# A new order in the prologue of an attention and FFN kernel, with identity matmuls on TensorE beside it

## The reference

```
x = x + attention(layernorm(x), ctx, ctx, WQ, WK, WV, WO, mask)
x = x + ffn(layernorm(x), W1, b1, W2, b2)
layernorm(x) = (x - mean) / sqrt(var + 1e-5)
attention: Q = x.WQ, K = ctx.WK, V = ctx.WV; softmax(Q.K / 8 + mask * -1e9).V; heads side by side, times WO
ffn: gelu(qlinear(y, W1, b1)), then qlinear(., W2, b2)
qlinear: activations rounded to 8 bits by their global minimum and maximum, weights by their largest magnitude
```

## Time and profile before

| | |
|---|---|
| median of three runs | 1129.66 us |
| the profiled execution's own time | 1126.18 us |
| its span, first to last instruction | 1124.1 us |
| mean granted clock of TensorE | 0.977 |
| busy: TensorE, DVE, ScalarE, POOL | 1018.1, 978.2, 865.1, 770.6 us |
| busy in 5 to 22 us of the prologue (17 us): TensorE, DVE, ScalarE, POOL | 4.91, 11.88, 7.66, 4.20 us |

### The profile page before, as it was taken

One profiled execution on the slowest core, in us unless ns is written; L12 is line 12 of the kernel. 1 busy time (PEld: TensorE's weight loads), 2 busy tenths in 40 slices (PEclk: granted clock), 3 DMA queues, 4 the chain that ended last, 5 costly groups with the idle time before them and its releaser, 6 DMA issues.

```text
span 1124.1 us, 37431 instructions
## 1 busy us (share of the span) xinstructions
PE 1018.1 (91%) x10489; PEld 643.3 (57%) x10489; DVE 978.2 (87%) x2528; ACT 865.1 (77%) x1805; POOL 770.6 (69%) x1108
## 2 busy tenths in 40 slices
PE   3999999999999999999999999999999999985808
PEld 2555566666666666666666666666666666653307
DVE  5777999999999999999999999999999999973997
ACT  4555888888888888888888888888888888873916
POOL 2246877777777777777777777777777777773700
PEclk9999999999999999999999999999999999996969
DMA  8301665555555555555555555555555555555003
GB/s 253 113 1 31 130 134 131 131 135 135 135 135 131 130 135 132 130 131 134 135 135 135 135 135 135 132 130 130 134 135 135 132 130 130 134 132 153 1 0 117
DMA packets 441419, 138.22 MB, mean 123 GB/s; under 512 B 413650, under 2 KB 440374, under 8 KB 441398
## 3 DMA queue, kind: packets, MB, share of 16 engines
q1 hardware_dynamic: 441398, 137.96, 51.0%
HBM read 28.60 MB, written 6.55 MB: 31 GB/s over the span
## 4 chain that ended last, share of the span: by engine, by line
PE 75%; DVE 10%; ACT 5%; issue 4%; POOL 3%; DMA 1%; DVEq 1%; ACTq 0%; SPq 0%; POOLq 0%
PE front L341 19%; PE front L343 17%; PE front L342 17%; PE back L1226 8%; PE front L1208 6%; PE tp L1208 5%; POOL hl L585 3%; DVE hrange L1059 2%; DVE hrange L1060 2%; DVE prob L939 2%; ACT prob L711 2%; DVE k_l L959 1%; ACT q_h L749 1%; PE front L1291 1%; ACT ctx_h L745 1%
## 5 line engine op out<-in xcount | busy, mean ns | idle before, releaser
L585 POOL TENSOR_TENSOR hl<-prob,hl 100x361 f16<-100x361 f32 x512 | 432.1, 853 | 97.2 <-DVE hl L946 50.9
L711 ACT ACTIVATE prob<-prob,nmax 100x361 f32<-100x361 f32 x512 | 293.9, 587 | 47.7 <-DVE nmax L939 47.5
L341 PE MATMUL front<-ctx_h,wk_h 128*128 128x362 f16 x512 | 164.2, 321 | 31.3 <-POOL ctx_l L574 17.8
L1226 PEld LDWEIGHTS back<-v,pT 128*128 128x128 f16 (+1 forms) x4608 | 165.1, 98 | 45.1 <-issue 9.6
L717 ACT ACTIVATE hl<-prob 100x361 f16<-100x361 f32 x352 | 176.0, 500 | 7.9
L1226 PE MATMUL back<-v,pT 128*128 128x65 f16 (+1 forms) x4608 | 174.2, 194 | 6.3 <-DMA pT<-hl 6.2
L343 PE MATMUL front<-ctx_h,wk_l 128*128 128x362 f16 x512 | 161.7, 316 | 0.0
L342 PE MATMUL front<-ctx_l,wk_h 128*128 128x362 f16 x512 | 161.5, 315 | 0.0
L721 ACT ACTIVATE k_h<-front 128x362 f16<-128x362 f32 x256 | 118.9, 464 | 54.7 <-PE front L343 54.7
L959 DVE SCALAR_TENSOR_TENSOR k_l<-front,k_h 128x362 f16<-128x362 f32 x256 | 135.2, 528 | 24.4 <-ACT k_h L721 21.8
L939 DVE CUSTOM_DVE_ANT_0 prob<-front,mask_g,ngain 100x361 f32<-100x361 f32 x256 | 149.6, 584 | 2.2
(11 more groups left out here) (180 smaller groups left out, 1980.8 us busy)
## 6 DMA issues: line engine op xcount, KB each, us to landing
ctx_raw<-ctxT SPq DMA_DIRECT2D x33, 361.0 KB, 3.1
pT<-hl SPq DMA_TRANSPOSE x256, 3.1
xs<-x SPq DMA_DIRECT2D x8, 400.0 KB
q_all<-x SPq DMA_DIRECT2D x32, 100.0 KB
out<-q_all SPq DMA_DIRECT2D x32, 100.0 KB
xb<-out SPq DMA_DIRECT2D x5, 640.0 KB, 7.5
out<-xb SPq DMA_DIRECT2D x25, 128.0 KB, 1.8
q_all<-wq SPq DMA_DIRECT2D x1, 1024.0 KB, 6.6
```

Source lines behind the costliest of these rows:

```text
L341: eng.matmul(dst, lh, rh, start=first, stop=False)
L585: pool.tensor_tensor(hl[0:T, n % RT, 1, 0:S], prob[0:T, n % RP, 0:S], hl[0:T, n % RT, 0, 0:S], ALU.subtract).then_inc(s_lo, 1)
L711: act.activation(prob[0:T, n % RP, 0:S], prob[0:T, n % RP, 0:S], ACT.Exp, bias=nmax[0:T, n:n + 1], scale=-1.0).then_inc(s_exp, 1)
L1226: ins = pe.matmul(obank[j % 2][:, n % GH * DV:(n % GH + 1) * DV], pT[0:r, n % RT, part_ * ST + st, :], v2[half][0:r, st, v, n % HT, :], st ...
```

## The change

DVE's instructions at the start of the prologue get another order: the maxima of WQ and its unit come in front of chunk 1's statistics, and x's low halves in front of WQ's first low half. TensorE gets 128 more matmuls of the float16 identity by itself, 128 columns each, into bank `tp[1]`, which nothing uses until chunk 1: 80 ahead of the transposes of chunk 0, 8 ahead of `top_w(0)`, 24 behind it, and 16 more once the first high half of WQ is there. Nothing reads what they write. The other engines' code is unchanged.

```diff
@@ DVE @@
         stats_x(0)
         dve.wait_ge(s_st, TB)
         ln_moments(chain(dve, s_lv), dve, 0)
-        stats_x(1)
         abs_w(0, 0)
         abs_w(0, 1)
         unit_w(0)
-        low_w(0, 0)
+        stats_x(1)
         start(dve, (s_k, s_v, s_cm, s_cr, s_sv, s_max, s_mg, s_hv, s_ri, s_nrm, s_x1, s_ln))
         x_low(0, 0)
+        low_w(0, 0)
         low_w(0, 1)
         stats_x(2)
@@ TensorE @@
+        def warm_up(times):
+
+            for _ in range(times):
+                pe.matmul(tp[1][:, 0:P], identb[:, :], identb[:, :], start=True, stop=True)
+
+        warm_up(80)
         x_transposes(0, 0)
+        warm_up(8)
         top_w(0)
+        warm_up(24)
+        pe.wait_ge(s_whi, 1)
+        warm_up(16)
         for c in range(NB):
             q_chunk(c, c % 2, c < NB - 1)
```

## The result

The changed kernel takes 1130.63 us (median of 20 runs, 1128.71 to 1132.09), the kernel before 1129.0 us in 20 runs beside them. The ratio is 1.0018 (95% interval 1.001 to 1.0025): it is slower, by 1.6 us as the difference of the medians and 2.0 us by the ratio. That is clear of zero; the ratio lies just inside the 0.2% that the prediction took as its bound, and its interval reaches beyond it. The profiled execution has a span of 1128.6 us and a mean granted clock of 0.974, against 1124.1 us and 0.977 before. About half of this difference of the clocks is one of bookkeeping: over the first 30 us the column has 0.94 after and 1.00 before, though the rows of before show nine matmuls at the low level there.

A forecast was written before the change was run, and what follows sets the result against it. TensorE's chain of waits (75%) bounds the kernel, so its exit from the prologue counts: 1.0 (m = 2 later) + 1.9 (clock) = +2.9 us, +2.3 against the median 1129.66, giving 1132.0 us; 8 in 10 from 1128.9 to 1133.9.

The forecast's parts named there:

- the rival given 0.13: Clock low at chunk 0's transposes: maximum at 14.6 instead of 13.3, m = 2 1.3 us later, 1133.3 us; chance 0.13.
- POOL held: POOL's steps for chunk 1 blocked beside WQ's two low halves on DVE, ending at 21.1 instead of 19.2 alone.
- The four terms of the prediction's sum: POOL's last four steps for chunk 1, 0.28 + 0.28 + 1.11 + 0.2 us from 19.1, said to end at 21.1.
- the upper bound of 22.35: Latest end of POOL's steps for chunk 1, if x's low halves on DVE block POOL too.
- m = 2: Projection's third output block, waits for ScalarE's copy of block 0: 0.8 to 1.1 us later than 22.80, taken 1.0.
- The clock falls: TensorE's clock falls in its 3.8 us wait before m = 2, costing 1.45 to 2.7 us, taken 1.9.
- the row of 4.09 us: Old profile: TensorE stood 4.09 us before a matmul at 1010.81, and the granted clock had fallen by then.
- not blocked enough: POOL ends at 19.2, TensorE waits 2.0 us and keeps its clock, m = 2 1.05 us earlier, 1128.0 us; chance 0.12.
- the luck of the profile of before: Profiled old prologue had an early clock rise; otherwise it loses up to 1.2 us more, 0.6 in the middle.
- the forecast's case: POOL blocked, m = 2 1.0 us later, clock falls in the wait for 1.9 us: 1132.0 us; chance 0.55.
- The case with the clock held: POOL blocked but TensorE's clock holds in the wait: only 1.0 us lost, 1130.1 us; chance 0.17.
- the gain arrives whole: TensorE starts projection 1.6 us earlier at full clock, 3.1 us gained, copy of block 0 by 19.8, 1126.0 us; chance 0.03.

The follow-up runs named there:

- experiment 1: Only the identity matmuls added to the kernel before, DVE's order as before; 1126.58 us, ratio 0.9985 to the kernel before.
- experiment 3: Changed kernel with 60 more identity matmuls ahead of m = 2, in TensorE's wait; 1130.24 us, ratio 1.0016 to the kernel before.
- Experiment 5: Changed kernel with WQ's low halves on DVE reading one input from a zeroed PSUM tile instead of SBUF; 1126.75 us, ratio 0.9984 to the kernel before.
- experiment 4: Changed kernel with chunk 1's statistics moved between WQ's maxima and WQ's unit on DVE; 1125.6 us, ratio 0.9976 to the kernel before.
- experiment 2: Changed kernel without any identity matmuls, so DVE's new order alone; 1130.59 us, ratio 1.0019 to the kernel before.
- experiment 6: Changed kernel with chunk 1's statistics ahead of WQ's unit and no identity matmuls; 1127.35 us, ratio 0.9992 to the kernel before.

## Why the prediction was right, step by step

1. **WQ's maxima** from 8.2 to 10.5: measured 8.23 to 10.57.
2. **80 matmuls** between 4.3 and 8.5 us, hidden: 6.91 us, to 8.95, 2.8 us ahead of the transposes. They raise the clock.
3. **The scale** ready at 14.15: its reciprocal ran from 14.02 to 14.18. This rests on the fast clock at the transposes (0.91 us). The clock was high there in both profiles of the changed kernel. In those of experiments 1, 3 and 5 it had fallen by the transposes of the maxima (0.63 to 0.69 us instead of 0.39), and in that of experiment 4 just behind them; so the rival given 0.13 does occur, in part, in kernels whose TensorE has the same work up to there (experiments 3 and 5); how often it does in the changed kernel itself is not known.
4. **Statistics** at 14.1 to 15.5: 14.10 to 15.48.
5. **Projection** from 17.75: 17.77. WQ's low halves were done at 18.83 (18.9).
6. **POOL held** beside the low halves, shift at 21.1: it ended at 21.13. The agreement to 0.03 us is luck. The four terms of the prediction's sum, from 19.1, give 20.97 and not 21.1. Three steps were done in front of the first held one, not four, so one more step of 0.28 us stood behind the low halves; and POOL went on from 18.97, 0.13 us earlier than taken. x's low halves let POOL through: three steps from 15.56 to 16.33 ran beside them at 0.20 to 0.21 us, so the upper bound of 22.35 falls and the Trainium skill's rule agrees here too. Experiment 5 shows the mechanism, with 1.98 us for the hold; the forecast's own difference was 1.9 us (21.1 less 19.2).
7. **m = 2** 1.0 us later: 0.88 later (22.80 to 23.68).
8. **The clock falls** with the wait: shown. Price taken 1.9 us, measured 1.68 us (3.72 less 2.04, experiment 3), or 1.69 against the kernel before's own 2.03. One of the two rows from which the fall was argued was misread. The row at 1020.85 was taken as a clock that held through 2.27 us, but it was low before that wait (columns as in the earlier trace rows):

```profile
1017.00:1018.00 1.00, 1.00 (x7) 0.95 (x6) 0.00 (x0) 0.09 (x1) 0.67 (x1) 0.50 0.00 0
...
1019.00:1020.00 1.00, 0.00 (x0) 0.00 (x0) 0.11 (x1) 0.00 (x0) 0.00 (x0) 1.00 0.83 190
```

It rose at about 1018.9, in the wait itself, and the row says nothing of a clock that holds. The rows that do are in the new profiles: behind a wait of 2.81 us the transposes of the changed kernel still ran at the high level (0.91 us), and so did m = 2 behind 1.73 us in experiment 5. The forecast's choice between fall and hold thus stood on the row of 4.09 us alone, and the kept clock in the price of the rival "not blocked enough" had no row behind it.

The sum against the profile: 0.88 + 1.69 = 2.57 us, where 2.9 was forecast, and it passes the loop whole. (The spans of the two profiles differ by 4.5 us; the rest is 0.2 us in the loop and 1.7 us behind it.) **Mis-sized terms.** Both of the above by 0.1 and 0.2 us; and the luck of the profile of before, taken as 0.6 us. The second profile of before is 1.58 us later at chunk 1's transposes, so half of this, 0.8 us, is the better figure. At L821 the means of two profiles each are 95.75 before and 97.34 after: 1.6 us. That is also the measured difference of the medians, where 2.3 was forecast; with two profiles of each kernel, and stretches behind the loop that differ by up to 3 us, so close an agreement is partly luck. The rest of the 1.4 us between 1132.0 and 1130.63 is the starting point: 1129.66 was the median of three runs, and 20 runs have 1129.0.

The chances: the forecast's case came true in its mechanism, and the result lies just under the bound of 0.2% that split this case between same and slower. The case with the clock held fell with the rows behind m = 2 in both profiles of the changed kernel. The case "not blocked" fell with the rows of POOL; "the gain arrives whole" needed the statistics earlier on DVE and the copy of block 0 by 19.8; experiment 4 gives it both, and has 5.8 us at L821 against the changed kernel.

The prediction's sentence that all of the gain is lost in the wait is borne out by experiments 1 and 2: the matmuls are worth 1.3 us at L821 with the old order (against the first profile of before), 1.9 to 2.0 us where POOL gets its input early, and 0.2 us in the changed kernel.

## What to carry to other kernels

When a step of one engine is moved ahead of another, the step that was passed now runs beside new neighbours: ask who waits for it and what will run beside it, since small steps of POOL took 1.26 and 1.11 us instead of 0.20 beside DVE instructions with two SBUF inputs. A gain at the start of TensorE's work is only kept if the next tile that it must wait for comes earlier too, and a wait of 3.7 us cost another 1.7 us through the clock. Put the small producer of a long chain (statistics, POOL, ScalarE) in front, and only then the long work.

## What had not been expected of the hardware

- Executions of one program differ by the moments at which TensorE's clock rises: 1.6 us in the prologue of the kernel before and, together with a lower clock, 3.1 us behind its loop, as large as the whole effect of the change. The profile's own time (1126.18 before) was an early rise, and the same parts in several profiles were needed to read the change.
- Identity matmuls meant to keep the clock up grow long when it has fallen: 40 of them took 4.47 us in experiment 1 and 4.02 us in experiment 4, and ended only 0.10 and 0.37 us ahead of the projection. Neither time did they delay it.
- 12 semaphore increments of DVE took 0.99 us where they stood behind a short instruction (experiments 4 and 6).
- The clock rose inside one wait of TensorE (at 1018.9 in the kernel before) and fell just behind another (at 23.9 in the changed kernel), so the matmuls on both sides of a wait have to be read.
